# Per-chunk statistics ahead of attention, and three last-layer programs made into two, in a two-layer Mamba, attention and experts kernel

## What is computed

```python
q = (x @ Wqa @ Wqb).reshape(b, s, H, D)          # 256 -> 64 -> 256, 16 heads of 16
kv = (x @ Wkva @ Wkvb).reshape(b, s, KVH, D, 2)  # 256 -> 32 -> 128, 4 heads
q = _rope(q); k = _rope(k)
...
out = out @ Wout + bout
...
scores = jnp.einsum('BTC,CE->BTE', x, gate_w)    # 8 experts
probs = jax.nn.softmax(scores, axis=-1)
top_p, top_idx = jax.lax.top_k(jnp.transpose(probs, (0, 2, 1)), cap)   # cap = 256 tokens of 1024
xin = jnp.take_along_axis(x[:, None, :, :], top_idx[..., None], axis=2)
h = jax.nn.gelu(jnp.einsum('BElC,ECH->BElH', xin, w1), approximate=False)
y = jnp.einsum('BElH,EHC->BElC', h, w2) * top_p[..., None]
out = jnp.zeros((B, T, C), x.dtype).at[b_idx, top_idx].add(y)
```

## Time and profile before

| | us |
|---|---|
| median of 3 runs (2592.0 to 2594.71) | 2592.47 |
| the profiled execution | 2589.91 |
| its span | 2588.2 |
| PE busy in it | 2270.5 (88%) |
| DVE busy | 1793.5 (69%) |
| ACT busy | 1338.4 (52%) |
| POOL busy | 1336.6 (52%) |

### The profile page before, as it was taken

How to read it: one execution, slowest core, us unless ns; L and a number is a source line. 1 busy time by engine, 2 the same in 40 slices (tenths; PEclk the granted TensorE clock), 3 DMA queues, 4 the chain that set the end, 5 groups by cost and what they waited for, 6 DMA issues and landing times. The chain is left out here.

```text
span 2588.2 us, 35369 instructions
## 1 busy us (share of the span) xinstructions
PE 2270.5 (88%) x11484; PEld 1338.2 (52%) x11485; DVE 1793.5 (69%) x2757; ACT 1338.4 (52%) x2573; POOL 1336.6 (52%) x1010
## 2 busy tenths in 40 slices
PE   8995988989989986899956699999998449999998
PEld 3342444545545543799943344444445226666666
DVE  6998999999999997555545888888884641112200
ACT  5777888787877774322214456666665111111110
POOL 1545999898898893577746322222221013333332
PEclk9997999999999998899977799999999669999999
DMA  5458244134133115544454612222200322333322
GB/s 162 148 187 268 103 138 162 49 107 138 49 129 117 49 48 167 121 72 72 71 112 85 142 33 33 44 38 34 33 3 20 114 91 65 82 66 69 75 51 25
DMA packets 149682, 231.18 MB, mean 89 GB/s; under 512 B 26257, under 2 KB 98897, under 8 KB 149394
## 3 DMA queue, kind: packets, MB, share of 16 engines
q1 hardware_dynamic: 119202, 189.20, 24.0%
q0 software_dynamic: 30336, 40.16, 9.6%
HBM read 152.23 MB, written 81.66 MB: 90 GB/s over the span
## 5 line engine op out<-in xcount | busy, mean ns | idle before, releaser
L1263 POOL TENSOR_TENSOR scan_hC<-scan_h,scan_c_all 128x1024 f32<-128x1024 f32 x256 | 612.4, 2415 | 65.4 <-DVE scan_h L1118 64.2
L1118 DVE TENSOR_TENSOR_SCAN scan_h<-scan_dA,banks 128x1024 f32<-128x1024 f32 x224 | 504.6, 2276 | 21.3 <-ACT scan_dA L1040 12.9
L893 PE MATMUL banks<-scan_hC,all_ident 128*128 128x512 f32 x1024 | 486.9, 600 | 26.4 <-DVE scan_xc L1125 26.4
L2392 ACT ACTIVATE attn_pt<-banks 128x1024 f32<-128x1024 f32 (+3 forms) x384 | 292.3, 811 | 186.4 <-PE banks L2339 185.2
L1033 ACT ACTIVATE scan_scaled<-mamba_duT,mamba_bT 128x128 f32<-128x128 f32 x1024 | 312.0, 387 | 20.9 <-PE banks L870 20.4
L2276 POOL TENSOR_SCALAR_AFFINE_SELECT attn_pt<-attn_pt 128x256 f32<-128x256 f32 x256 | 103.6, 411 | 383.9 <-ACT attn_pt L2392 382.2
L2410 DVE TENSOR_REDUCE attn_m_lo<-banks 128x1 f32<-128x512 f32 (+3 forms) x432 | 266.8, 662 | 30.4 <-PE banks L2295 19.9
L893 PEld LDWEIGHTS banks<-scan_hC,all_ident 128*128 128x128 f32 x1024 | 185.5, 192 | 179.3 <-issue 129.2
L3066 DVE TENSOR_TENSOR ffn_y<-banks,ffn_gates 128x512 f32<-128x512 f32 x32 | 22.1, 692 | 357.1 <-PE banks L2965 350.4
L2902 POOL DMA_INDIRECT out<-ffn_y,ffn_ids x64 | 101.0, 1577 | 297.6 <-DVE ffn_y L3066 287.8
L2295 PE MATMUL banks<-attn_K,attn_Q 96*128 96x512 bf16 (+3 forms) x768 | 231.8, 340 | 11.5 <-DVE attn_mask L2404 10.7
(11 more groups left out here) (337 smaller groups left out, 3857.8 us busy)
## 6 DMA issues: line engine op xcount, KB each, us to landing
scan_c_all<-scratch_bc SPq DMA_DIRECT2D x64, 512.0 KB, 6.0
ffn_w<-in_e_w SPq DMA_DIRECT2D x16, 1024.0 KB, 4.9
attn_Q<-scratch_q SPq DMA_DIRECT2D x96, 128.0 KB, 4.1
scratch_x<-front_xc SPq DMA_DIRECT2D x8, 1024.0 KB, 5.8
scratch_z<-front_zs SPq DMA_DIRECT2D x8, 1024.0 KB, 7.6
scan_xc<-scratch_x SPq DMA_DIRECT2D x16, 512.0 KB, 3.6
scan_zs<-scratch_z SPq DMA_DIRECT2D x16, 512.0 KB, 4.6
scratch_dt<-front_lw SPq DMA_DIRECT2D x7, 1024.0 KB, 4.1
```

The lines of the kernel that those rows point to most:

```text
L893: mm = pe.matmul(PS[:, YB + i, :], ident[:, :], hC[:, u % NHC, i * BANK:(i + 1) * BANK], start=s == 0, stop=s == NST - 1, skip_group_check ...
L1118: dve.tensor_tensor_scan(h[:, u % NH, :], decay, drive, 0.0, ALU.mult, ALU.add).then_inc(scanned, 1)
L1263: pool.tensor_tensor(hC[:, u % NHC, :], h[:, u % NH, :], c_all[:, s, :], ALU.mult).then_inc(hC_done, 1)
L2392: act.activation(pt[:, at % 4, 2 * pair:2 * pair + 2, 0:width], PS[:, ST + 2 * pair:ST + 2 * pair + 2, 0:width], ACT.Exp, scale=HD ** -0.5 ...
```

## The change

**Projection stage.** Statistics are made chunk by chunk. The second table's rows of chunks 0 and 1 are loaded by SP with plain DMAs into the still unused tile `proj_rq` and added by DVE; POOL's adding DMAs remain for chunks 2 to 7, and two of them are issued earlier. `chain` is cut in two (`chain_to_var`, `chain_to_nmr`), and inside step q DVE works on chunk q+3: up to the variance between `by_cos` and `join` (the two halves of `rope`), the rest behind `join`. ACT takes the root of chunk q+3 in step q, and the root of chunk 1 ahead of `copy_low(0)`. SP's load of chunk c waits for the addition of chunk c-2 instead of c-4.

**Out-projection.** `project_scores` replaces `project_layernorm` and the products of `expert_probs`. Statistics go in groups of 16, 8, 4 and 4 tiles; normalising is shared by ACT, POOL and, for two tiles, DVE; ACT makes all but one of the copies of turned pairs; twelve of the sixteen pairs are turned inside the projection loop (six before). The gate scores are two rounds inside the same block.

```diff
+        GROUPS = [(0, 16), (16, 24), (24, 28), (28, 32)]
+        BY_ACT = list(range(0, 24, 2)) + [24, 25, 28, 29]
+        BY_POOL = list(range(1, 24, 2)) + [26, 27]
+        BY_DVE = [30, 31]
+        OWNERS = ((xn_act, BY_ACT), (xn_pool, BY_POOL), (xn_dve, BY_DVE))
+        ROOT_AT = {17: 0, 25: 1, 29: 2}
+        NORM_AT = {18 + i: t for i, t in enumerate(range(0, 16, 2))} | {26 + i: t for i, t in enumerate(range(16, 24, 2))}
+        TURN_AT = {20 + p: p for p in range(PAIRS - 4)}
+        COPY_AT = {22 + p: p for p in range(PAIRS // 2 + 2)}
...
+                if t in TURN_AT:
+                    turn_xn(TURN_AT[t])
+            score(0)
+            turn_xn(PAIRS - 4)
+            turn_xn(PAIRS - 3)
+            by_token(0)
+            turn_xn(PAIRS - 2)
+            turn_xn(PAIRS - 1)
+            score(1)
+            by_token(1)
```

**Choice and lists.** `choose_experts` holds the softmax, the choice and the experts in one block. The weights' loads stand at its start. In the digit loop the update of the level and the next digit's candidates are made behind the comparisons:

```diff
-            for k in range(DIGITS):
-                dve.tensor_tensor(trial[:, :, :, :].rearrange("p c b e -> p c (b e)"),
-                                  level[:, None, :, :].rearrange("p c b e -> p c (b e)").to_broadcast(tries),
-                                  digit_i[:, k, :, None].to_broadcast(tries),
-                                  ALU.bitwise_or).then_inc(leveled, 1)
-                dve.wait_ge(leveled, 5 * k + 1)
-                for half in range(2):
-                    at = slice(half * HI, (half + 1) * HI)
-                    dve.tensor_tensor(above[:, :, :, at, :], by_batch[:, None, :, at, :].to_broadcast(cut),
-                                      trial[:, :, :, :].bitcast(F32)[:, :, :, None, :].to_broadcast(cut),
-                                      ALU.is_ge).then_inc(tried, 1)
...
-                dve.tensor_tensor(level[:, :, :], level[:, :, :], digit[:, :, :], ALU.bitwise_or).then_inc(leveled, 1)
+            dve.tensor_copy(flat3(grown), digit_i[:, 0, :, None].to_broadcast(tries)).then_inc(leveled, 1)
+            for k in range(DIGITS):
+                dve.wait_ge(leveled, 6 * k + 1)
+                dve.tensor_tensor(flat3(trial), flat3(grown), each(digit), ALU.bitwise_or).then_inc(leveled, 1)
+                dve.wait_ge(leveled, 6 * k + 2)
+                for half in range(2):
+                    at = slice(half * HI, (half + 1) * HI)
+                    dve.tensor_tensor(above[:, :, :, at, :], by_batch[:, None, :, at, :].to_broadcast(cut),
+                                      trial[:, :, :, :].bitcast(F32)[:, :, :, None, :].to_broadcast(cut),
+                                      ALU.is_ge).then_inc(tried, 1)
+                dve.tensor_tensor(level[:, :, :], level[:, :, :], digit[:, :, :], ALU.bitwise_or).then_inc(leveled, 1)
+                dve.wait_ge(leveled, 6 * k + 3)
+                if k + 1 < DIGITS:
+                    dve.tensor_tensor(flat3(grown), each(level), digit_i[:, k + 1, :, None].to_broadcast(tries),
+                                      ALU.bitwise_or).then_inc(leveled, 1)
+                else:
+                    dve.memset(grown[:, :, :, :], 0).then_inc(leveled, 1)
+                dve.wait_ge(counted, k + 1)
+                dve.tensor_scalar(kept[:, :, :, :].rearrange("p c b e -> p (c b e)"), PS[:, 0, 0:TRIALS * NL], float(CAP),
+                                  digit_f[:, k:k + 1], ALU.is_ge, ALU.mult).then_inc(leveled, 1)
+                dve.wait_ge(leveled, 6 * k + 5)
+                dve.tensor_tensor(kept[:, 0, :, :], kept[:, 0, :, :], kept[:, 1, :, :], ALU.add).then_inc(leveled, 1)
+                dve.wait_ge(leveled, 6 * k + 6)
+                dve.tensor_tensor(digit[:, :, :], kept[:, 0, :, :], kept[:, 2, :, :], ALU.add).then_inc(leveled, 1)
...
+            def mark(e, b):
+                spread = [P, TPB, P]
+                dve.tensor_tensor(onehot[:, b % 2, :, :], lanes[:, None, :].to_broadcast(spread),
+                                  lane[:, b * TPB:(b + 1) * TPB, bass.ds(e, 1)].to_broadcast(spread),
+                                  ALU.is_equal).then_inc(onehot_made, 1)
...
-                    for i in range(TPB):
-                        op = dve.tensor_scalar(onehot[:, b % 2, i, :], lanes[:, :], lane[:, b * TPB + i, bass.ds(e, 1)], None,
-                                               ALU.is_equal)
-                    op.then_inc(onehot_made, 1)
...
-            for e in range(2):
-                lists(e, e == 0)
+            first_lists(0)
+            first_lists(1)
+            lists(1, False)
...
             for hp in range(UH):
                 up(0, 0, 0, hp, True)
+                lists(1, hp, True)
+                if 0 < hp <= KC:
+                    turn(0, 1, hp - 1, True)
```

The core of the projection's part:

```diff
-        GROUPS = [(0, 1), (1, 2), (2, 4), (4, 6), (6, NCH)]
+        GROUPS = [(c, c + 1) for c in range(NCH)]
+        AHEAD = 3
...
-            load_x(0)
-            load_x(1)
+            for c in range(2):
+                load_x(c)
+                sp.dma_start(odd_rows(c), odd[:, c * TC:(c + 1) * TC, :]).then_inc(odd_in[c], 16)
+            load_x(2)
             loads.start(sp)
...
                 if q < NCH:
-                    rope(q)
-                if q in (0, 2):
-                    chain(3 + q // 2)
+                    by_cos(q)
+                if q + AHEAD < NCH:
+                    chain_to_var(q + AHEAD)
+                if q < NCH:
+                    join(q)
+                if q + AHEAD < NCH:
+                    chain_to_nmr(q + AHEAD)
```

727 lines of the change are left out of this document (377 added, 350 removed).

## The result

The changed kernel took 2564.3 us (median of 4 runs, 2561.5 to 2565.3), the kernel before 2592.2 (2590.6 to 2594.7); the ratio is 0.9889, with a 95% interval of 0.9877 to 0.9901. That is 27.9 us shorter. The two profiled executions have spans of 2588.2 and 2563.5 us, so they are 24.7 us apart: the changed kernel's profile is of the slowest of its four executions (2565.3), that of before is of an execution (2589.9) shorter than the four behind its median. The table cuts both at the same events; a stretch is the difference of two starts in the timelines.

The account below looks back on a forecast made before the run. PE bounds the experts' loop, so gains lie ahead of it, where PE waits. Terms -14.6 - 6.9 - 3.2 - 6.5 = -31.2 us take the profiled 2589.9 to 2558.7, against the median 2561; range 2550 to 2575.

Parts of the forecast that it names:

- A: Projection ahead of attention: an earlier first `proj_qk` and shorter steps, minus 14.6 us, between 0 and minus 24.
- B: Out-projection and scores, to the first trial level: minus 6.9 us, between minus 3 and minus 9.
- D: From lanes to experts: first product 10.6 us sooner, 4.1 given back between products; minus 6.5, between minus 2 and minus 9.
- A, head: Projection's start: root's wait minus 5.8 us, chunk 1's normalising minus 5.3; first `proj_qk` 11.1 sooner, at 1358.
- bound by its transfers: Rival, projection's head: chunk 3's load and weights come as late as 1357, gain only 5.8 us, 2570; chance 0.15.
- A, pace: Projection's seven steps: 73.0 us instead of 76.5, minus 3.5, bounds minus 12 and plus 4.
- the ring: Projection steps 0 to 4: `turn`, `join`, `chain_to_nmr` and normalising release one another in a circle, 12 us a step.
- ACT as the bound: Rival, out-projection: ACT at 1.8 us a step, last product 3 us later, gain 3.9, total 2564; chance 0.12.
- C: Digits: the level's update leaves the chain, 2.72 us a digit instead of 2.95; minus 3.2, between 0 and minus 3.4.
- halves one after another: Rival, multiplications behind the lanes: DVE's and POOL's halves run in turn, 5.5 us instead of 3.3, total 2563.7; chance 0.10.
- The other side: Rival, experts' loop: PE waits for wide comparisons if one takes over 3.9 us; 5.2 would eat the gain; chance 0.03.

Follow-up runs that it names:

- e8: Changed kernel with VectorE's `chain_to_nmr` ahead of `join` in the projection's steps, as before the change; 2565.5 us.
- e7: Changed kernel with ScalarE's root of chunk q+3 in the projection's steps moved behind the copies of the second parts; 2560.8 us.
- e11: Changed kernel with VectorE's statistics of chunk q+3 at the start of projection steps 2 to 4; 2563.6 us.
- e12: Changed kernel with the edits of e5, e6 and e10, plus earlier statistics and reciprocal and a later root in projection steps 2 to 4; 2554.3 us.
- e5: Changed kernel with TensorE's wait for the gate's weights moved from the out-projection's first turned tile to the first round of scores; 2563.3 us.
- e6: Changed kernel with ScalarE's second and third out-projection roots, and the normalisings behind them, one tile later; 2562.7 us.
- e4: Changed kernel with the digits' loop of the kernel before; 2565.4 us.
- e9: Changed kernel with each batch's one-hots made by eight narrow comparisons instead of one wide one; 2563.2 us.
- e10: Changed kernel with all multiplications by VectorE, the second half between the two first lists, none by GpSimd; 2562.5 us.
- e2: Changed kernel with the projection of the kernel before, so only the later stages' changes; 2576.4 us, ratio 0.9942 to the kernel before.

## Why the prediction was right in the sum and wrong in places

The time came 3 us over the forecast and inside the range, though two steps failed, and part of that nearness is luck. The terms were read from one profile and add up to -31.2, and the two profiles are 24.7 apart, so the terms missed by 6.5: 1.7 in A, 3.6 in B, 0.2 in D and 1.0 in stretches that no edit touches. That the medians are 27.9 apart is the scatter of executions, which came to the forecast's help.

**A, head.** Right in mechanism: ScalarE's root has no idle time ahead of it (-5.8), VectorE's addition took 1.23 us (1.2 assumed), the statistics of chunk 0 began 6.9 us after the load (7.1). Too small in one size: I had the first `proj_qk` 11.1 us sooner, it came 13.7 sooner. Chunk 3's load, from 188 GB/s, was put at 17 us after the stage's start; GpSimd issued behind it at 14.8. The 188 was a mean over a stretch of before and no limit: the head now moves twice that (last section). The rival "bound by its transfers" is out for the same reason; the DMA share that spoke for it rose from 0.85 to 1.00 while the head became 13.7 us shorter.

**A, pace: the step that failed.** "A ring appears in steps 0 to 4" through `turn`, `join`, `chain_to_nmr` and normalising, 12 us a step. The size was near (13.5, 13.3, 12.7, 12.5) by luck, the place was wrong, and the two last steps, 10.4 and 7.3 where I had 7.9 each, were too. I priced the ring's operations too high (`join` 2.8 for 1.56, `turn` 4.1 for 3.1, normalising 4.4 for 3.6); at their measured lengths the ring needs 8.9 and doesn't set the step. e8 takes `join` out of it with no effect, which alone would not decide, since normalising grew to 4.79 there. What sets a step is the loop shown above, with the other loop right behind it (e7, e11, e12), and in the first of them PE's clock, for which I had no term. I had also written that ACT's long stalls go; of 14.4 us in two of them (8.14 and 6.26) 13.3 were still there, spread over five roots. So the seven steps grew by 1.5 us where I had -3.5. 5.1 less gain here, 2.6 more in the head and a tail 0.8 shorter (22.3 against 23.1 behind the last chunk's first copy) make A -12.9 instead of -14.6.

**B: the second step that failed.** -3.3 instead of -6.9. The last product ended 49.0 us after the stage's first load; I had 43.9 (2009.6 - 1965.67). The steps with pairs took the 1.52 expected. Missing were the gate's wait, which the scores brought to the head of PE's program (e5: 2.4, of it some 0.5 by the clock), and ScalarE's stops at the roots 1 and 2, its second and third, behind which a copy of PE's next tile stands (e6: 2.9); together they are the 5.1, within the runs' scatter. In e12, without both, it is 44.0. The prediction asked what is queued behind a waiting instruction only for the root ahead of `proj_qk`. The way from the last product to the first trial was 1.4 shorter than costed (14.1 against 15.5). ACT as the bound, as that rival had it, did not come: it kept up wherever it had no variance to wait for.

**C.** Right, -3.2, and e4 by itself 2.9, or 2.6 with the copy ahead of the first trial, which falls into B's stretch. Two errors of 0.3 at most: VectorE's idle time ahead of the count is 0.20, not 0.1, as part of the displaced operations overlap, and the first digit took 3.56, its level update 0.66 instead of 0.18: GpSimd makes the scores' parts beside it.

**D.** -6.1 counted from the first multiplication, -6.5 predicted. Ids nearly right (done 7.4 us behind the first multiplication, I had 7.1). From ids to turned rows 8.9, not 7.1: "the same four gathers" are not the same beside wide comparisons (e9). Experts' first product therefore at 19.95 and not 18.0. In exchange the experts' stretch grew only by 2.4 of the 4.1 that I gave to the lists and turns in it. That stretch is 475.2 to 476.7 in all runs with the changed experts, 1.5 us of scatter, so no more is to be read from it.

The multiplications came out at 3.2 where I had 3.3, for a wrong reason. I let VectorE lose half of what it could lose to GpSimd. It needs 1.6 alone (e10), not 1.9, and then waited for one of GpSimd's operations in each of three. Both halves together took 4.0 us (2068.32 to 2072.35), not the 5.5 of the rival "halves one after another", since GpSimd's half, which I had priced at 3.6, adds only 2.4 to VectorE's 1.6. So the two engines take turns and the rival's mechanism is the one the runs show, at a smaller price. By the rule of the Trainium skill (SBUF — State Buffer, section "SBUF: two separate sides") a VectorE operation with two SBUF inputs and a GpSimd one that reads SBUF share a pair of ports, which goes to whichever starts first for its whole instruction. The trace agrees: 0.98 us beside GpSimd, 0.55 alone.

**The other side** did not come: in the experts' loop PE didn't wait for one-hots, and a wide comparison took 1.2. (Its product groups are 3.6 us apart, 28.53 / 8, not the 3.4 that I wrote.)

Left open: how much of the head's 10.3 us is the smaller groups' and how much the root's new place; which of B's and D's edits, among merged blocks, turned pairs inside the loop and wide comparisons, gave how much of their gain, since e2 has them all together; how much of a step is PE's clock; and how long the steps would be with GpSimd's `turn` on another engine, which was not tried.

## What to carry to other kernels

When you merge stages, list for each engine what its program now waits for ahead of its first useful instruction: a wait that was at its own stage's start may stand before work that doesn't need it. When you divide a statistics chain so that one engine no longer waits in it, look for the loops that are left and price each from its own rows. Of two of nearly one length, cutting one gives little: here the seven steps fell by 2.9 us (e7), 0.2 (e8) or not at all (e11), and by 3.7 with both cut (e12). The second shows in the trace only when the first is shorter. Work split between VectorE and GpSimd may be worth no more than the two take in turn: measure one half alone before you split.

## What the runs showed of the hardware

- VectorE and GpSimd held one another up by whole instructions, whatever the size, but not in all operations. A VectorE operation of 4 elements a partition took 1.6 us beside one `turn` instead of 0.16 (e12), another 4.06 across two (e11, at 1381.80), `by_cos` 4.49 (at 1369.98 in the changed kernel) instead of 1.47, and four normalisings 6.04 instead of 2.18. Not longer were VectorE's operations on a bank of PE's results (`proj_rest<-banks`, 0.69 us beside GpSimd and without it) and the statistics of a tile (0.41 in both cases).
- The clock came back at different times behind equal work. In all fourteen profiles PE stopped 1.9 us ahead of the out-projection's first load; in the changed kernel and seven others with the same order of instructions there the mean granted clock from 4 to 8 us behind that load was 0.50 to 0.59, in e7 0.83, and its out-projection was 1.2 us shorter.
- GpSimd's issue of an indirect gather took 2.03 and 1.87 us beside a wide comparison with two inputs from SBUF, 1.10 and 0.98 beside narrow ones with one.
- In the projection's head the DMA engines moved 341 to 387 GB/s for 6.6 us on end. The row of rates of the changed kernel from 1335 to 1357, in 40 slices of 0.55 us:

```profile
GB/s 0 0 0 0 67 115 298 344 378 387 372 357 352 358 346 352 350 344 341 286 189 120 33 55 168 337 317 192 134 171 186 199 125 162 156 155 201 199 183 359
```
